# Filler matmuls ahead of TensorE's waits in the later stages of a two-layer hybrid kernel

## What is computed

```python
x = x + softmax_attention(layernorm(x))    # n = 0: causal, 16 heads of 8 channels
x = x + expert_ffn(layernorm(x))           # n = 1: 8 experts, top 2, and a shared network
x = x + feature_attention(layernorm(x))    # n = 2: "the second attention", 16 heads, 32 random features
x = x + expert_ffn(layernorm(x))           # n = 3
x = x + gated_scan(layernorm(x))           # n = 4: decaying state, 8 heads of 64
x = x + fp4_ffn(layernorm(x))              # n = 5: "the first fp4 network"
x = x + retention(layernorm(x))            # n = 6
x = x + fp4_ffn(layernorm(x))              # n = 7: "the second fp4 network"
```

## Time and profile before

| | |
|---|---|
| median of 3 runs | 1064.11 us (1063.82 to 1064.73) |
| span of the profiled execution, which has no other time of its own | 1065.4 us |
| instructions | 16468 |
| mean granted clock of TensorE over the span | 0.918 |
| PE busy | 921.6 us (87%) |
| DVE busy | 773.7 us (73%) |
| ACT busy | 410.8 us (39%) |
| POOL busy | 349.1 us (33%) |
| chain of work that ended last | PE 61%, DVE 29%, issue 4% |
| second attention | about 370 to 485 us of the span |
| first fp4 network, retention, second fp4 network | about 822 to 892, 889 to 985 and 984 to 1065 us |

### The profile page before, as it was taken

One profiled execution on the slowest core, in us unless ns is written; L12 is line 12 of the kernel. 1 busy time (PEld: TensorE's weight loads), 2 busy tenths in 40 slices (PEclk: granted clock), 3 DMA queues, 4 the chain that ended last, 5 costly groups with the idle time before them and its releaser, 6 DMA issues.

```text
span 1065.4 us, 16468 instructions
## 1 busy us (share of the span) xinstructions
PE 921.6 (87%) x6039; PEld 533.2 (50%) x6039; DVE 773.7 (73%) x1837; ACT 410.8 (39%) x678; POOL 349.1 (33%) x446
## 2 busy tenths in 40 slices
PE   7889999899999987788999994798999678989666
PEld 3434444443444566563444441455667456767344
DVE  5668888767666466778676669757666998788985
ACT  2525556554323334343433347132222334321232
POOL 6362323222313344332342330322121344333333
PEclk9899999999999968779999997799999889986897
DMA  5363121201000000000000000000000000000000
GB/s 133 105 157 99 47 69 59 71 24 82 1 1 1 1 1 2 1 2 0 1 1 1 0 1 1 3 1 1 1 1 1 1 1 1 2 1 2 0 11 30
DMA packets 11532, 24.34 MB, mean 23 GB/s; under 512 B 1323, under 2 KB 7635, under 8 KB 11315
## 3 DMA queue, kind: packets, MB, share of 16 engines
q1 hardware_dynamic: 11152, 22.30, 7.3%
q10 hardware_dynamic: 294, 0.91, 0.3%
HBM read 15.69 MB, written 7.34 MB: 22 GB/s over the span
## 4 chain that ended last, share of the span: by engine, by line
PE 61%; DVE 29%; issue 4%; POOL 2%; ACT 2%; DMA 1%; DVEq 0%; SPq 0%; POOLq 0%; ACTq 0%
PE ps L1058 5%; PE ps L1065 4%; PE ps L1053 4%; PE ps L412 4%; PE ps L362 3%; PE ps L2705 2%; PE ps L2106 2%; PE ps L382 2%; DVE a_MN L542 2%; PE ps L2103 2%; DVE XN L159 2%; PE ps L2445 2%; DVE g_C L1862 2%; PE ps L1352 2%; PE ps L938 2%
## 5 line engine op out<-in xcount | busy, mean ns | idle before, releaser
L542 DVE TENSOR_REDUCE a_MN<-ps 128x1 f32<-128x384 f32 (+3 forms) x154 | 93.2, 636 | 27.1 <-PE ps L365 25.4
L1281 POOL TENSOR_TENSOR f_Y<-f_Y,f_TT 128x512 f32<-128x512 f32 x48 | 60.9, 1269 | 131.9 <-DVE f_TT L1137 131.9
L666 ACT ACTIVATE a_PT<-ps 128x1024 f32<-128x1024 f32 x56 | 57.3, 1024 | 61.9 <-PE ps L382 61.7
L1229 ACT ACTIVATE f_HH<-ps,pack_zero 128x512 f32<-128x512 f32 x64 | 44.0, 687 | 94.7 <-PE ps L1053 94.7
L112 POOL TENSOR_TENSOR rs<-t,mhalf 128x4 f32<-128x4 f32 x36 | 37.1, 1031 | 129.6 <-DVE t L95 128.1
L1058 PE MATMUL ps<-f_XS,pack_zero 128*128 128x512 f32 x128 | 73.0, 652 | 0.0
L1137 DVE SCALAR_TENSOR_TENSOR f_TT<-ps,pack_zero,f_X 128x512 f32<-128x512 f32 x64 | 47.8, 746 | 33.6 <-PE ps L1065 33.2
L1065 PE MATMUL ps<-f_HH,pack_zero 128*128 128x512 f32 x128 | 66.1, 598 | 5.0 <-DVE f_TT L1137 5.0
L1053 PE MATMUL ps<-f_XS,pack_zero 128*128 128x512 f32 x128 | 67.3, 607 | 0.7 <-DVE f_XS L1021 0.7
L362 PE MATMUL ps<-a_KS,a_QS 72*128 72x128 bf16 (+3 forms) x224 | 54.1, 305 | 9.0 <-DVE a_MN L542 8.0
L1021 DVE TENSOR_TENSOR f_XS<-ps,XNT 128x512 f32<-128x512 f32 x64 | 43.7, 685 | 17.3 <-PE ps L938 15.2
(11 more groups left out here) (334 smaller groups left out, 2206.3 us busy)
## 6 DMA issues: line engine op xcount, KB each, us to landing
scratch<-a_parts SPq DMA_DIRECT2D x16, 384.0 KB, 3.8
a_QS<-scratch SPq DMA_DIRECT2D x14, 288.0 KB
a_KS<-scratch SPq DMA_DIRECT2D x42, 96.0 KB
pack_one<-in_one SPq DMA_DIRECT2D x1, 2694.5 KB, 10.3
pack_zero<-in_zero SPq DMA_DIRECT2D x3, 884.5 KB, 4.6
X<-in_x SPq DMA_DIRECT2D x4, 256.0 KB, 10.0
out_x<-X SPq DMA_DIRECT2D x4, 256.0 KB, 2.0
a_QS<-a_MT SPq DMA_DIRECT2D x42, 4.0 KB
```

The costliest lines, as they stand in the source:

```text
L542: dve.tensor_reduce(M.a_MN[:, n % 2, ti, h0:h0 + k], bank(M, M.bank["a_max", n, jj], 128 * (ti + 1) * k).rearrange("p (a c) -> p a c", a=k ...
L666: act.activation(M.a_PT[:, c % 8, 0:1024], M.ps[:, a * 512:a * 512 + 1024], ACT.Exp).then_inc(made.sem, made.tick(n, hh))
L1281: pool.tensor_tensor(M.f_Y[:, i, :], M.f_Y[:, i, :], M.f_TT[:, u % 3, :], ALU.add).then_inc(made.sem, made.tick(n, u))
```

## The change

A helper `filler(pe, M, bk, count)` is added. It takes the bank `bk` (which the code already took at that place, or takes soon after) and issues `count` matmuls of the bf16 identity `M.identb` by 512 columns of the bf16 constants `M.half` into it. Nobody reads the results: the next real matmul into the bank starts with `start=True`. No filler signals a semaphore. The helper is called ahead of waits for operands, between the taking of the bank and the wait. 117 fillers are issued: 42 in the second attention, 24 in the first fp4 network, 20 in retention and 31 in the second fp4 network with the last output product of retention in it. Nothing else changes on any engine. Where a bank is taken earlier than before (bank 4 ahead of `queries` and in `down`, bank 2 in `queries(b - 1, 2)`), the wait for its event moves ahead too.

```diff
+def filler(pe, M, bk, count):
+
+    take(pe, M, bk)
+    for _ in range(count):
+        pe.matmul(bank(M, bk), M.identb[:, :], M.half[:, 0:512], start=True, stop=True)
...
-def turn_tensor(pe, S, M, n, b, bk, src, ready):
+def turn_tensor(pe, S, M, n, b, bk, src, ready, fill=0):
 
     turned = S["transposed"]
-    take(pe, M, bk)
+    filler(pe, M, bk, fill)
     pe.wait_ge(ready[0].sem, ready[0].at(*ready[1]))
...
         bk = spare("p_sq", b, w)
+        if b == 0 and w == "k":
+            filler(pe, M, bk, 4)
         pe.wait_ge(S["p_sq"].sem, S["p_sq"].at(b, w))
...
             take(pe, M, 2 + g)
+        if b == 0 and w == "k" and pair[0] == 0:
+            filler(pe, M, 2, 2)
         pe.wait_ge(S["p_qt"].sem, S["p_qt"].at(b, w))
...
-        turn_tensor(pe, S, M, n, b, spare(), M.XN, (S["normed"], (n, b)))
+        turn_tensor(pe, S, M, n, b, spare(), M.XN, (S["normed"], (n, b)), 3)
...
         if b:
+            filler(pe, M, 4, (0, 4, 6, 2)[b])
             queries(b - 1, 0)
...
             sums_turned(b - 1)
+            if b >= 2:
+                filler(pe, M, 2, 4)
             queries(b - 1, 2)
...
     sums_turned(3)
+    filler(pe, M, 6, 3)
     heads(3)
     features_output(pe, S, M, 2, 3)
     turn_choice(pe, S, M, 3, 0, spare())
+    filler(pe, M, 0, 4)
...
+FILL = {5: (8, 5, 2, 5, 2, 0, 0, 0), 7: (8, 4, 2, 2, 2, 2, 3, 2)}
...
         turned, tiles = S["q_turned"], (2 * u, 2 * u + 1)
+        filler(pe, M, 4, FILL[n][u])
         pe.wait_ge(S["q_hq"].sem, S["q_hq"].at(n, u))
...
         if u == 6:
-            turn_tensor(pe, S, M, n, 3, 5, M.XM, (S["x_quant"], (n, 3)))
+            turn_tensor(pe, S, M, n, 3, 5, M.XM, (S["x_quant"], (n, 3)), 2)
         elif u == 4 and n == 7:
-            turn_tensor(pe, S, M, 7, 2, 5, M.XM, (S["x_quant"], (7, 2)))
+            turn_tensor(pe, S, M, 7, 2, 5, M.XM, (S["x_quant"], (7, 2)), 1)
...
     M.bank["r_out", b] = bk
-    take(pe, M, bk)
+    filler(pe, M, bk, 3 if b == 3 else 0)
...
         bk = spare("r_mean", b, k)
+        filler(pe, M, bk, 0 if k else 3)
...
-        turn_tensor(pe, S, M, n, b, other(), src, ready)
+        turn_tensor(pe, S, M, n, b, other(), src, ready, 2)
```

## The result

| | before | changed |
|---|---|---|
| median | 1065.34 us (9 runs, 1063.65 to 1069.91) | 1056.71 us (9 runs, 1050.42 to 1062.28) |
| span of the profiled execution | 1065.4 us | 1048.6 us (its own time 1050.42 us) |
| mean granted clock, profiled execution | 0.918 | 0.947 |

The ratio of the changed kernel to the one before is 0.9896, 95% interval 0.9873 to 0.9920: 8 to 14 us faster, 11 us by the ratio and 9 by the medians. The forecast was 22 us, and 1042 us with a range of 1029 to 1056. The direction was right, the gain half of the forecast, and the median lies just above the range.

A forecast was written before the change was run, and what follows sets the result against it. TensorE's clock falls after short waits, 129.7 us at the lower level. Terms of 29.9 us, less 2.9 and 2.5 for remaining falls and 2.4 for fillers, give 22 us: 1064.1 to 1042 us, range 1029 to 1056.

The forecast's parts named there:

- The fillers' cost: Whole change: 32 fillers lie in no wait, 7.0 us; TensorE alone sets the pace for about 11, so 2.4 us charged.
- What the clock gives back: Touched stages: each low stretch saves the smaller of 0.42 x TensorE busy and length less VectorE busy; together 29.9 us.
- the stretch at 374.2: Start of the second attention: a held clock saves 5.6 us of the 20.5 us low stretch, capped by VectorE.
- the one at 422.0: Second attention, `b = 2`: a held clock saves 3.2 us, 0.42 of TensorE's busy time.
- The term of 445.9: Second attention, `b = 3`: a held clock saves 5.6 us, 0.42 of TensorE's busy time.
- the prediction's cap: All low stretches: none can become shorter than VectorE's busy time in it; 5.6 us at 374.2, 0.3 us at 855.5.
- the terms of `b = 2` and `b = 3`: Second attention, the longest waits: a third of both terms, 2.9 us, lost to remaining falls; 2.5 us for the rest.
- the falls move: Rival, chance 0.15: filler runs only shift the gap, the clock falls elsewhere in the stage; 10 us saved, 1054 us.
- Only long waits bring a fall: Rival, chance 0.05: fillers in waits under 2 us do nothing; 1062 to 1067 us, no change.
- Slower: Rival, chance 0.08: clock stays low and the 32 uncovered fillers cost 14 us, 1078 us, or 7 us, 1071 us.
- VectorE isn't in the way: Rival, chance 0.12: some VectorE work moves into neighbouring waits, so stretches shrink further; about 1031 us.
- The rule on transposes: Fp4 networks: transposes don't count as clock activity, so the last fp4 terms, some 3 us, are lost; 1045 us.

The follow-up runs named there:

- narrow fillers: All 117 fillers at 32 x 32 of the array instead of 128 x 128, same 512 columns; ratio to the kernel before 1.0018, median 1071.46 us.
- uncovered ones alone: Kernel before plus only the 32 fillers that the prediction found in no wait; ratio to the kernel before 1.0025, median 1068.01 us.
- kernel with 72 fillers: Fillers in no wait left out, those in long waits lengthened, none in the fp4 networks or retention's last product; ratio to the kernel before 0.9907.
- longer runs: Changed kernel with filler runs in the 1.7 to 5.2 us waits made as long as the waits, 205 fillers; ratio to the kernel before 0.9837.
- fp4-only kernel: Kernel before plus only the 55 fillers of the two fp4 networks and retention's last product; ratio to the kernel before 0.9987, median 1067.04 us.
- trimmed kernel: Changed kernel without the 32 fillers that the prediction found in no wait, 85 left; ratio to the kernel before 0.9846, median 1051.79 us.

## Why the prediction was half right

**The mechanism was right.** Fillers keep the clock up, and what is behind them runs faster. The narrow fillers, which change the array's work and nothing else, lose the whole gain.

**The fillers' cost was right.** 2.4 us were charged; the uncovered ones alone cost 2.7 us (0 to 5), and 117 that hold nothing up 2 us by the ratio and 5 by the medians.

**What the clock gives back was right on the whole, with one term far off.** The terms were 29.9 us for 129.7 us of low clock, 0.23 us each. In the traces the second attention gave 8.1 us for 37.5 and retention 3.8 us for 20.5, 0.22 and 0.19. In the 61 runs of the kernel before, whose clock scatters by itself, a line through time against low time (twice one minus the clock, times the span) rises by 0.31 us for each us. Two terms can be read alone, where a trace has no low clock left: the stretch at 374.2 gave 5.8 us (5.6 were forecast), and the one at 422.0, in the kernel with 72 fillers, whose 16 fillers fill the wait at `b = 2` but for 0.64 us, shortens its part from 14.95 to 11.68 us, 3.3 us (3.2 forecast).

The term of 445.9, 5.6 us, was far too high. In the changed kernel its part of the program, up to the end of the second attention, gained 0.7 us for 10.2 us less low clock, and in the kernel with 72 fillers 1.7 us for 20.5. The saved time is lost again at VectorE's normalisation for the next block (timelines of VectorE, before and changed, and of PE, changed):

```profile
467.99 1.23 DVE L159 TENSOR_SCALAR XN<-X,mv,rs 128x128 f32<-128x128 f32 x4
```

```profile
453.70 3.15 DVE L166 TENSOR_SCALAR XN<-X,mv,rs 128x128 f32<-128x128 f32 x4 [0.56 <-POOL rs L128]
```

```profile
456.91 1.11 PE L181 MATMUL ps<-pack_first,XN 128*128 128x128 f32 x4 [3.00 <-DVE XN L166]
```

VectorE now comes to it 0.56 us before GpSimd has finished `rs`, and the four instructions take 3.15 us instead of 1.23, the first two 2.58 and 1.46 us instead of 0.65 and 0.47. In the seven traces in which VectorE starts them right behind GpSimd's `rs` and beside its addition to `X` they take that long, and in the other six that are compared here, the one before among them, they don't. TensorE then waits 3.00 us, and the fall at 456.2 lies in that wait. So the prediction's cap, VectorE's busy time of before, left out GpSimd. Whether the slow instructions come from sharing something with GpSimd was not tested.

**The step that failed** is how many falls go. The prediction held that of the 29.9 us only a third of the terms of `b = 2` and `b = 3`, 2.9 us, and 2.5 us for the rest would be lost, 18% in all. The median clock of the nine runs is 0.940 against 0.916, which is 127 us of low clock against 179: 52 us went, where the 24.5 us of the sum stood for 106. At 0.23 to 0.31 us each, 52 us are 12 to 16, less 2.4 to 2.7 for the fillers: 9 to 14 us, and 11 were measured by the ratio, 9 by the medians. Even the mildest execution, the profiled one, kept 68 of the 130 us in the touched stages, over half. The sentence that had it, that six fillers leave 2.8 of the 4.09 us empty and eight leave 3.5 of the 5.24, was read as a reason for a third off. It was the reason for most of it at `b = 2`, where the clock fell behind the 2.80 us (411.8) and 6.8 of 10.2 us stayed, and for all of it at `down(0)` of the second fp4 network, where 10.2 us of low clock stand in place of 3.4 (timeline of PE, changed kernel):

```profile
986.93 1.89 PE L79 MATMUL ps<-pack_half 128*128 128x512 bf16 x8
992.33 1.54 PE L2481 MATMUL ps<-pack_first,q_HQ 128*128 128x128 f32 x6 [3.51 <-POOL q_HQ L2669]
```

The rival "the falls move" had 0.15 and 1054 us; it was the nearest, and in the first part of the second attention it is what most traces show. The longer runs show that the early end of the fillers is a cause: with the waits filled nearly to their ends the clock is 0.958 and 7 to 9 us more come, and at `b = 2` the fall goes with the wait.

**The other rivals.** "Only long waits bring a fall" is out: the six fillers in waits of 0.84 and 1.80 us take away 6.8 to 20.5 us of the 20.5 us stretch in every trace that has them in full size. This is against the Trainium skill's rule on short gaps, page "TensorE: Matmul & The Clock Gate", section "Why this matters for your kernels". "Slower" is out. "VectorE isn't in the way" can't be judged, since no kernel held the clock throughout. Its price was added up wrongly: half of what lies between 29.9 and 47 is 38, but the same deductions are 5.4 + 2.4 = 7.8 us and not 5, which gives about 1033 and not 1031.

**The rule on transposes** of the Trainium skill, page "TensorE: Matmul & The Clock Gate", section "Part 4: PE-mode transpose", gave 1045. The fp4 terms were indeed not seen in the fp4-only kernel. But with longer runs ahead of the same transposes the fp4 fillers gave 7 us, so fillers do help there when they are long enough. Whether the transposes themselves hold the clock no run shows.

**What stays open.** The trimmed kernel is 0.9925 of the changed one, while the 32 fillers alone cost 0.0025; the difference, some 5 us, is inside the two intervals' sum but may be real, by falls that lie elsewhere. The same holds for the gains that don't add up. No run fixes where the falls lie, and so the two can't be separated. Nor is it shown why some short waits bring a fall and others don't: in the changed kernel's trace TensorE waits 1.74 us at 382.76 and 1.87 us at 406.79, and no fall stands between 370 and 411 us.

## What to carry to other kernels

A run of fillers has to last nearly until the operand comes; those that ended 1.57, 2.80 and 3.51 us early here left part of the fall or all of it in place (6.8 of 10.2 us behind the 2.80), and their own time is then spent for nothing or at double price. Fill the waits from their ends, by the trace of the kernel that has them, leave out every filler with no idle time under it, and check that a narrow filler of the same length does nothing. When a faster engine is to bring time, look which other engine it will then meet, as VectorE met GpSimd here. Judge such a change by many runs and by the granted clock of each, since a single trace can hold 4 us that come from stages that nobody touched.

## What the runs showed of the hardware

A bf16 product of 32 x 32 by 512 columns takes as long as one of 128 x 128 (1.03 against 1.04 us for four), and the clock falls behind the first and not behind the second, with 0.85 us empty behind either.

The clock stayed at 0.50 over 20.4 us at the start of the second attention with the narrow fillers, although TensorE was busy for 19.7 of them (windows of that kernel):

```profile
376.60:397.00 20.40, 19.73 (x146) 15.21 (x148) 14.43 (x31) 8.31 (x14) 9.92 (x8) 0.50 0.00 1
```

Where falls lie differs between executions of one program. The unchanged kernel's 61 runs have clocks of 0.904 to 0.922, the changed kernel's nine 0.934 to 0.947, and stages ahead of the first filler were up to 4.0 us shorter and 2.0 us longer than in the first trace.

One and the same VectorE instruction, the first normalisation of a 128 x 128 tile (`XN` from `X`, `mv` and `rs`) at the end of the second attention, took 0.65 us in six traces and 2.58 us in the seven in which it began within 0.1 us of an addition of 128 x 512 on GpSimd.

In one execution TensorE was busy 2339.1 us and not some 920, with `features` at 2.63 us against 1.16, at a granted clock of 1.0 throughout, while the busy times of VectorE, ScalarE and GpSimd were nearly the usual ones.
